# Attention loops of a graph network on one Trainium2 core: the turned logits are shown one round later

## Chip, cores, metric

The kernel runs on one core of one Trainium2 chip. The metric is the device time of one execution in microseconds (us). A run gives the median of several executions; the profiled execution is a separate one with its own time.

## What is computed

Four graph layers over 3125 nodes and 100000 edges sorted by destination, 256 features. The two layers that matter here are attention over the incoming edges of each node. GATv2 is applied twice (the stages `edges1` and `edges2`), GAT with four heads once (`gat_edges`):

```python
# _gatv2, for each edge src -> dst
h = jax.nn.leaky_relu(xl[src] + xr[dst] + eattr @ We, SLOPE)
logits = h @ att
m = jax.ops.segment_max(logits, dst, n)
ex = jnp.exp(logits - m[dst])
denom = jax.ops.segment_sum(ex, dst, n)
out = jax.ops.segment_sum(xl[src] * (ex / denom[dst])[:, None], dst, n)
...
# _L2_gnn_ref, 4 heads
e = jax.nn.leaky_relu(a_src[src] + a_dst[dst], NEG_SLOPE)
m = jax.ops.segment_max(e, dst, num_segments=N)
ex = jnp.exp(e - m[dst])
```

The other stages (a dense product of node pairs for the first and last layer, layer and batch norms, node projections) are untouched.

## The kernel before, in words

The edges are cut into windows of 512 (4 tiles of 128), and windows at block borders are visited twice, so that each of the 220 groups has edges into one block of 128 nodes. The two functions `gatv2_loop` and `gat_loop` run over these groups. Each engine runs its own program, and the engines meet at semaphores alone: one per kind of step, counted up once for each group.

A group passes through a chain of small steps, one of each per group t. Each engine does them in rounds: in round s it takes its steps in a fixed order, each for the group t = s - lag. The list of (lag, step) pairs, handed to `pipelined` (a hardware loop of ten rounds, on TensorE and ScalarE) or to `straight` (written out, on VectorE), sets that order. A step that has to wait stops all that stands behind it on its engine.

In `gatv2_loop` the chain of a group is:

- GpSimd: `gather`, four indirect DMAs (L942) that fetch the source rows of a group into a ring of ten buffers. Before group t it waits for `group_sum` of group t - 10.
- ScalarE: `place` (L1040, L1043) and `mask` (L1050) make the one-hot matrix of destinations and an offset for absent places.
- TensorE: `mix` (L1082, L1085), 16 bf16 matmuls that sum the destination's and the edge's terms.
- VectorE: `sum_inputs` (L954), `dot` (L961), `add_linear` give the logits; `high_part` to `low_part` (L1018) split them into three bf16 parts.
- TensorE: `turn_parts` (L1066), one matmul that transposes the parts. ScalarE: `copy_turned` (L1030), the cast into `rows`.
- TensorE: `show_logits` (L1093, L1095), five matmuls that lay the logits of the group out as nodes by edges in PSUM.
- VectorE: `see` (L967), the maximum of each node, `raise_top`, `drop`, `set_top`. ScalarE: `exponentials` (L1056, L1058).
- TensorE: `flip` (L1072), four fp32 transposes. ScalarE: `copy_weights` (L1034).
- TensorE: `sum_group` (L1104), fp32 matmuls of weights and gathered rows, which also wait for `add_group` of the group before. VectorE: `add_group` (L1013).

ScalarE's order in a round is copy_turned, copy_weights, place, mask, exponentials. `gat_loop` has the same plan with four heads: `mask_first_heads` and `mask_last_heads` (L1367), `turn_parts` (L1361), `show_logits` (L1381, 16 matmuls), `bring_top` (L1355), `mix` (L1409), `flip` (L1390), `sum_group` (L1400) on TensorE; on ScalarE `copy_turned` (L1303), `shrinkage` (L1343), `weigh_late` (L1317), `mask`, `choose` (L1338), `exponentials` (L1308), `weigh_early` (L1317); its gather is L1162.

Of the kernel before, what the change touches and what calls it, by code (L numbers as in the profile page):

```python
# [130 lines left out]
def blocks_on(nc, m, engine):  # L131

    def load(first, n, turn):
        _, values = nc.values_load_multi_w_load_instructions(
            m.tab[0:1, bass.ds(first, n)], engines=[engine], min_val=0, max_val=NB,
            skip_runtime_bounds_check_because="the list of groups has blocks 0 to NB only")
        return values
    return load
# [753 lines left out]
def gatv2_loop(nc, m, name, table, c):  # L892
# [7 lines left out]
    with stage_of(nc, name) as (st, block):  # L900
# [48 lines left out]
        def _(dve):  # L949
# [66 lines left out]
            def low_part(t, u, turn, b):  # L1016
# [1 line left out]
                nc.vector.tensor_tensor(lo, m.rest[:, 0:T], md, ALU.subtract).then_inc(parts, 1)  # L1018


            straight([(2, sum_inputs), (2, dot), (3, see), (2, add_linear), (5, add_group), (3, raise_top),
                            (2, high_part), (3, drop), (2, without_high), (3, set_top), (2, middle_part),
                            (2, low_part)], blocks_on(nc, m, mybir.EngineType.DVE))
            dve.wait_ge(done, NG)

        @block.scalar
        def _(act):
            def copy_turned(t, u, turn, b):
                act.wait_ge(turned, t + 1)
                nc.scalar.copy(rows, turn_ps[:, 0:P]).then_inc(copied, 1)  # L1030

            def copy_weights(t, u, turn, b):
                act.wait_ge(flipped, t + 1)
                nc.scalar.copy(m.prob[:, 0, :], flip_ps[:, :]).then_inc(weights, 1)  # L1034

            def place(t, u, turn, b):
                r = u % R
                act.wait_ge(arrived[r], 16 * n_loads * nth(u, turn, R))

                nc.scalar.activation(m.locrow[r][:, :], m.locrow[r][:, :], ACT.Abs,  # L1040
                                     bias=m.minus_icol[:, 0:1]).then_inc(distance, 1)
                act.wait_ge(distance, t + 1)
                nc.scalar.activation(m.ohT[r][:, :], m.locrow[r][:, :], ACT.Relu, scale=-1.0,  # L1043
                                     bias=m.one[:, 0:1]).then_inc(placed, 1)

            def mask(t, u, turn, b):
                r = u % R
                act.wait_ge(placed, t + 1)

                nc.scalar.activation(m.off[r][:, :], m.ohT[r][:, :], ACT.Identity, scale=BIG,  # L1050
                                     bias=m.minus_big[:, 0:1]).then_inc(masked, 1)

            def exponentials(t, u, turn, b):
                r = u % R
                act.wait_ge(raised, t + 1)
                nc.scalar.activation(m.expT[:, :], shown_ps[:, :], ACT.Exp, bias=m.new[:, 0:1]).then_inc(exps, 1)  # L1056
                act.wait_ge(dropped, t + 1)
                nc.scalar.activation(m.less[r][:, 0:1], m.drop[:, 0:1], ACT.Exp).then_inc(shrink, 1)  # L1058

            pipelined(act, [(3, copy_turned), (4, copy_weights), (0, place), (1, mask), (3, exponentials)])  # L1060

        @block.tensor
        def _(pe):
            def turn_parts(t, u, turn, b):
                pe.wait_ge(parts, t + 1)
                nc.tensor.matmul(turn_ps[:, 0:P], m.parts[:, :], m.ident_bf[:, :], start=True,  # L1066
                                 stop=True).then_inc(turned, 1)

            def flip(t, u, turn, b):
                pe.wait_ge(exps, t + 1)  # L1070
                for j in range(T):
                    mm = nc.tensor.transpose(flip_ps[:, j * P:(j + 1) * P], m.expT[:, j * P:(j + 1) * P], m.ident[:, :])  # L1072
                mm.then_inc(flipped, 1)

            def mix(t, u, turn, b):
                r, q = u % R, u % 2
                pe.wait_ge(placed, t + 1)
                after(pe, summed, t, 2)
                for j in range(T):
                    e = slice(j * P, (j + 1) * P)  # L1080
                    for s in range(3):
                        nc.tensor.matmul(zb[q][:, j, :], m.ohT[r][:, e], blk(m.xr3, b, s * D, (s + 1) * D),  # L1082
                                         start=(s == 0), stop=False)

                    mm = nc.tensor.matmul(zb[q][:, j, :], m.eaT[r][:, e], m.We12[c][:, :], start=False, stop=True)  # L1085
                mm.then_inc(mixed, 1)

            def show_logits(t, u, turn, b):
                r = u % R
                pe.wait_ge(copied, t + 1)  # L1090
                pe.wait_ge(masked, t + 1)

                nc.tensor.matmul(shown_ps[:, :], m.ident_bf[:, :], m.off[r][:, :], start=True, stop=False)  # L1093
                for j in range(T):
                    mm = nc.tensor.matmul(shown_ps[:, j * P:(j + 1) * P], m.tilesel[:, j, :], rows,  # L1095
                                          start=False, stop=(j == T - 1))
                mm.then_inc(shown, 1)

            def sum_group(t, u, turn, b):
                r = u % R  # L1100
                pe.wait_ge(weights, t + 1)
                after(pe, done, t, 1)
                for j in range(T):
                    mm = nc.tensor.matmul(sum_ps[:, 0:WA], m.prob[:, 0, j * P:(j + 1) * P], m.gath[u % RG][:, j, 0:WA],  # L1104
                                          start=(j == 0), stop=(j == T - 1))
                mm.then_inc(group_sum, 1)

            pipelined(pe, [(3, turn_parts), (4, flip), (3, show_logits), (1, mix), (4, sum_group)],
                      blocks_on(nc, m, mybir.EngineType.PE))


def gat_loop(nc, m, name, table):
# [8 lines left out]
    with stage_of(nc, name) as (st, block):  # L1121
# [47 lines left out]
        def _(dve):  # L1169
# [115 lines left out]
            def add_group(t, u, turn, b):  # L1285
# [3 lines left out]
                nc.vector.tensor_tensor(acc, acc, sum_ps[:, 0:WA], ALU.add).then_inc(done, 1)  # L1289


            straight([(2, see), (4, rescale), (1, sum_parts), (2, raise_top), (3, take_top), (1, add_src), (2, top_high_part),
                            (3, sink), (1, leak), (2, drop), (3, bound), (1, high_part), (2, top_without_high),
                            (2, set_top), (1, without_high), (2, top_middle_part), (1, middle_part),
                            (2, top_low_part), (1, low_part), (0, place), (3, weigh), (4, add_group)],
                      blocks_on(nc, m, mybir.EngineType.DVE))
            dve.wait_ge(done, NG)

# [1 line left out]
        def _(act):  # L1300
# [39 lines left out]
            def shrinkage(t, u, turn, b):  # L1340
# [1 line left out]
                act.wait_ge(dropped, t + 1)  # L1342
                nc.scalar.activation(m.less[r][:, 0:H], m.drop[:, 0:H], ACT.Exp).then_inc(shrink, 1)  # L1343

            pipelined(act, [(2, copy_turned), (3, shrinkage), (4, weigh_late), (1, mask), (3, choose), (3, exponentials),
                            (3, weigh_early)])

        @block.tensor
        def _(pe):
# [54 lines left out]
            def mix(t, u, turn, b):  # L1404
# [3 lines left out]
                for j in range(T):  # L1408
# [1 line left out]
                                          blk(m.adst3, b, 0, 3 * H), start=True, stop=True)  # L1410
                mm.then_inc(mixed, 1)

            pipelined(pe, [(2, mask_first_heads), (2, turn_parts), (2, mask_last_heads), (2, show_logits), (3, bring_top),
                           (1, mix), (3, flip), (4, sum_group)],
                      blocks_on(nc, m, mybir.EngineType.PE))


# [544 lines left out]
```

## Time and profile before

| what | value |
|---|---|
| median of 3 runs | 6605.63 us (6604.21 to 6607.28) |
| the profiled execution, its own time | 6665.35 us |
| its span, first to last instruction | 6663.5 us |
| mean granted TensorE clock | 0.923 |
| busy: TensorE matmuls / weight loads | 4911.5 us (74%) / 3594.1 us (54%) |
| busy: VectorE / ScalarE / GpSimd | 4773.6 us (72%) / 3300.0 us (50%) / 3314.7 us (50%) |

Busy is the time in which an engine's records lie; the ends of TensorE's are modelled and not observed. In rows of a timeline the columns are: start in us from the span's start, duration in us, engine, line, operation, out<-in by the program's names, number of instructions merged; in brackets the idle time of the engine before it and what ended that, where the profile tells (`remote`: it doesn't; `issue`: no wait ended there). PE is TensorE, DVE VectorE, ACT ScalarE, POOL GpSimd.

### The profile page before, as it was taken

The page shows a single profiled execution, that of the slowest core. Times are in us where ns is not written, and L with a number is a line of the kernel's source. Part 1 is how long each engine was busy: PE and PEld are TensorE (multiplying, and loading weights), DVE is VectorE, ACT ScalarE, POOL GpSimd, SP SyncE. Part 2 cuts the span into 40 slices and gives each one's busy share as a digit, 9 for nine tenths or more (in the row PEclk, how much of TensorE's full clock was granted, in tenths as well). Part 3 has the DMA queues.
Part 4 walks back from the last instruction along what each step waited for, and adds up shares of the span by engine and source line. Part 5 has one row for each costly group of instructions (what it writes and reads, how often), then busy time and mean ns, then how long its engine had stood idle before and what let it go on. Part 6 is the DMA issues. An engine that isn't in the chain of part 4 may idle for free. (4 is left out here: it accounts for less than half of the span.)

```text
span 6663.5 us, 117090 instructions
## 1 busy us (share of the span) xinstructions
PE 4911.5 (74%) x29984; PEld 3594.1 (54%) x30319; DVE 4773.6 (72%) x18137; ACT 3300.0 (50%) x8374; POOL 3314.7 (50%) x3591
## 2 busy tenths in 40 slices
PE   4999999947777777765777777775477767676589
PEld 2444447816556656643566565563355544454378
DVE  8999992457767777675777767677588777888801
ACT  4777771035555555543555555555355555555510
POOL 3444446545555555535555555552355555555200
PEclk9999999979999999988999999998689898999899
DMA  2233347724444444412444444440333333333164
GB/s 57 62 92 101 111 119 287 287 62 103 105 105 104 104 105 105 104 42 74 105 106 104 104 105 105 104 105 22 88 99 98 96 97 93 95 101 98 51 157 112
DMA packets 606529, 695.56 MB, mean 104 GB/s; under 512 B 243043, under 2 KB 512656, under 8 KB 599802
## 3 DMA queue, kind: packets, MB, share of 16 engines
q0 software_dynamic: 128832, 362.75, 21.6%
q1 hardware_dynamic: 477370, 329.75, 18.3%
q14 instruction: 280, 2.29, 0.1%
q8 instruction: 47, 0.77, 0.0%
HBM read 589.91 MB, written 102.19 MB: 104 GB/s over the span
## 5 line engine op out<-in xcount | busy, mean ns | idle before, releaser
L942 POOL DMA_INDIRECT gath<-table,src_col x880 | 843.3, 958 | 637.3 <-issue 628.2
L942 POOL DMA_INDIRECT h<-table,src_col x880 | 844.9, 960 | 581.3 <-issue 581.3
L1082 PE MATMUL psum<-xr,ohT 128*128 x5280 | 906.7, 296 | 35.1 <-ACT ohT L1043 35.1
L1030 ACT CAST rows<-psum 128x128 bf16<-128x128 f32 x440 | 117.1, 266 | 1337.9 <-remote 847.7
L1241 DVE TENSOR_REDUCE seen<-psum 128x2 f32<-128x1024 f32 x440 | 532.0, 1223 | 282.4 <-remote 158.3
L669 DVE SCALAR_TENSOR_TENSOR xr<-xr,gath,psum 128x259 f32<-128x259 f32 x1440 | 683.3, 474 | 7.4 <-PE psum L655 4.1
L1162 POOL DMA_INDIRECT gath<-table,src_col x440 | 440.1, 1000 | 469.4 <-issue 340.2
L961 DVE SCALAR_TENSOR_TENSOR zs<-zs,mean 128x256 f32<-128x256 f32 x1760 | 643.9, 421 | 0.0
L1082 PEld LDWEIGHTS psum<-xr,ohT 128*128 128x128 bf16 x5280 | 542.2, 106 | 126.9 <-issue 36.7
L1162 POOL DMA_INDIRECT h<-table,src_col x440 | 436.7, 992 | 308.7 <-issue 308.7
L954 DVE TENSOR_TENSOR zs<-psum,gath 128x1024 f32<-128x1024 f32 x220 | 269.4, 1225 | 446.1 <-remote 371.0
L954 DVE TENSOR_TENSOR zs<-psum,h 128x1024 f32<-128x1024 f32 x220 | 269.4, 1225 | 367.1 <-remote 307.2
L1095 PE MATMUL psum<-rows,tilesel 128*128 128x128 bf16 x1760 | 179.9, 228 | 469.6 <-ACT rows L1030 450.3
L1085 PE MATMUL psum<-We,eaT 128*128 128x256 bf16 x1760 | 523.1, 297 | 0.0
L664 DVE TENSOR_SCALAR locrow<-psum,acc 128x128 f32<-128x128 f32 x1440 | 495.2, 344 | 0.3 <-POOL xr L605 0.3
L621 ACT ACTIVATE xr<-irow,gath 128x128 f32<-128x128 f32 x1440 | 460.1, 390 | 56.6 <-PEq L173 6.3
L655 PE MATMUL psum<-zs,locrow 128*128 128x259 f32 x1440 | 416.8, 414 | 71.4 <-DVE xr L669 21.9
L1104 PE MATMUL psum<-h,prob 128*128 128x257 f32 x1760 | 430.6, 388 | 48.2 <-DVE acc L1013 46.7
L1104 PE MATMUL psum<-gath,prob 128*128 128x257 f32 x1760 | 436.7, 393 | 15.4 <-DVE acc L1013 14.5
L1093 PEld LDWEIGHTS psum<-off,ident_bf 128*128 128x128 bf16 x440 | 42.3, 96 | 741.7 <-ACT rows L1030 736.8
L698 PE MATMUL psum<-h,xr 128*128 128x256 f32 x1900 | 416.2, 381 | 5.9 <-DMA xr<-pairs 5.9
L698 PEld LDWEIGHTS psum<-h,xr 128*128 128x128 f32 x1900 | 363.2, 191 | 57.8 <-DMA xr<-pairs 7.7
(328 smaller groups left out, 12200.0 us busy)
## 6 DMA issues: line engine op xcount, KB each, us to landing
locrow<-g_locb SPq DMA_DIRECT2D x660, 128.0 KB
pairs<-xr SPq DMA_DIRECT2D x640, 115.5 KB
xr<-pairs SPq DMA_DIRECT2D x13, 1716.0 KB
gath<-table,src_col POOLq DMA_INDIRECT x1320
h<-table,src_col POOLq DMA_INDIRECT x1320
xr<-pairs SPq DMA_DIRECT2D x25, 832.0 KB
acc<-pairs SPq DMA_DIRECT2D x12, 1716.0 KB
xr<-pairs SPq DMA_DIRECT2D x13, 1584.0 KB
```

What stands on the lines that cost most here:

```text
L621: ins = nc.scalar.activation(gap[u % 2][:, j, :], m.irow[:, :], ACT.Abs, bias=col(t["low"], t4 * 4 + j))
L664: nc.vector.tensor_scalar(pick[u % 8], numbers, t["key"][:, g:g + 1], None, ALU.is_equal).then_inc(keyed, 1)
L669: nc.vector.scalar_tensor_tensor(kept[:, u, 0:EXTRA + 3], kept[:, (u - 1) % HELD, 0:EXTRA + 3], t["same"][:, g:g + 1], m.ps[u % 4][:, 0:EX ...
L698: mm = nc.tensor.matmul(sums_of(m, hb), lhs(i, hb), m.h[:, db, :], start=False, stop=(db == NB - 1 and (hb % 2 == 1 or hb == n - 1)))
L942: pool.indirect_dma_start(m.gath[r][:, j, :], None, table, bass.IndirectOffsetOnAxis(m.src_col[r][:, j:j + 1], 0)).then_inc(gathered[r], 16)
L954: nc.vector.tensor_tensor(m.zs[q][:, :, :], zb[q], m.gath[u % RG][:, :, 0:D], ALU.add).then_inc(summed, 1)
L961: ins = nc.vector.scalar_tensor_tensor(m.zs[q][:, j, :], m.zs[q][:, j, :], 0.0, m.att_relu[:, :], ALU.max, ALU.mult, accum_out=m.dots[:, j ...
L1082: nc.tensor.matmul(zb[q][:, j, :], m.ohT[r][:, e], blk(m.xr3, b, s * D, (s + 1) * D), start=(s == 0), stop=False)
L1085: mm = nc.tensor.matmul(zb[q][:, j, :], m.eaT[r][:, e], m.We12[c][:, :], start=False, stop=True)
L1104: mm = nc.tensor.matmul(sum_ps[:, 0:WA], m.prob[:, 0, j * P:(j + 1) * P], m.gath[u % RG][:, j, 0:WA], start=(j == 0), stop=(j == T - 1))
L1162: pool.indirect_dma_start(m.gath[r][:, j, :], None, table, bass.IndirectOffsetOnAxis(m.src_col[r][:, j:j + 1], 0)).then_inc(gathered[r], 16)
L1241: ins = nc.vector.tensor_reduce(m.seen[:, 2 * q:2 * q + 2], m.psum[:, 2 * q:2 * q + 2, :], AX.X, ALU.max)
```

## The change

All steps from `show_logits` on are taken one round later on every engine, and on TensorE `turn_parts` moves behind `show_logits`: what is turned and cast in one round is shown in the next. In `gatv2_loop` `turn_parts` also moves behind `mix`, next to `sum_group`. ScalarE's and VectorE's orders within a round stay as they are; only the groups differ.

```diff
@@ gatv2_loop, VectorE @@
-            straight([(2, sum_inputs), (2, dot), (3, see), (2, add_linear), (5, add_group), (3, raise_top),
-                            (2, high_part), (3, drop), (2, without_high), (3, set_top), (2, middle_part),
+            straight([(2, sum_inputs), (2, dot), (4, see), (2, add_linear), (6, add_group), (4, raise_top),
+                            (2, high_part), (4, drop), (2, without_high), (4, set_top), (2, middle_part),
                             (2, low_part)], blocks_on(nc, m, mybir.EngineType.DVE))
@@ gatv2_loop, ScalarE @@
-            pipelined(act, [(3, copy_turned), (4, copy_weights), (0, place), (1, mask), (3, exponentials)])
+            pipelined(act, [(3, copy_turned), (5, copy_weights), (0, place), (1, mask), (4, exponentials)])
@@ gatv2_loop, TensorE @@
-            pipelined(pe, [(3, turn_parts), (4, flip), (3, show_logits), (1, mix), (4, sum_group)],
+            pipelined(pe, [(5, flip), (4, show_logits), (1, mix), (3, turn_parts), (5, sum_group)],
                       blocks_on(nc, m, mybir.EngineType.PE))
@@ gat_loop, VectorE @@
-            straight([(2, see), (4, rescale), (1, sum_parts), (2, raise_top), (3, take_top), (1, add_src), (2, top_high_part),
-                            (3, sink), (1, leak), (2, drop), (3, bound), (1, high_part), (2, top_without_high),
-                            (2, set_top), (1, without_high), (2, top_middle_part), (1, middle_part),
-                            (2, top_low_part), (1, low_part), (0, place), (3, weigh), (4, add_group)],
+            straight([(3, see), (5, rescale), (1, sum_parts), (3, raise_top), (4, take_top), (1, add_src), (3, top_high_part),
+                            (4, sink), (1, leak), (3, drop), (4, bound), (1, high_part), (3, top_without_high),
+                            (3, set_top), (1, without_high), (3, top_middle_part), (1, middle_part),
+                            (3, top_low_part), (1, low_part), (0, place), (4, weigh), (5, add_group)],
@@ gat_loop, ScalarE @@
-            pipelined(act, [(2, copy_turned), (3, shrinkage), (4, weigh_late), (1, mask), (3, choose), (3, exponentials),
-                            (3, weigh_early)])
+            pipelined(act, [(2, copy_turned), (4, shrinkage), (5, weigh_late), (1, mask), (4, choose), (4, exponentials),
+                            (4, weigh_early)])
@@ gat_loop, TensorE @@
-            pipelined(pe, [(2, mask_first_heads), (2, turn_parts), (2, mask_last_heads), (2, show_logits), (3, bring_top),
-                           (1, mix), (3, flip), (4, sum_group)],
+            pipelined(pe, [(3, mask_first_heads), (3, mask_last_heads), (3, show_logits), (2, turn_parts), (4, bring_top),
+                           (1, mix), (4, flip), (5, sum_group)],
```

TensorE in the hardware loop of `edges1`, before: from the sum of one group to the show of another, with the semaphores that each row waits for.

```order
L1104 MATMUL psum<-h,prob 128x257 [waits edges1_done,edges1_weights]
L1104 MATMUL psum<-h,prob 128x257 x3
L1066 MATMUL psum<-ident_bf,parts 128x128 [waits edges1_parts]
L1072 MATMUL psum<-ident,prob 128x128 [waits edges1_exps]
L1072 MATMUL psum<-ident,prob 128x128 x3
L1093 MATMUL psum<-off,ident_bf 128x512 [waits edges1_masked,edges1_copied]
L1095 MATMUL psum<-rows,tilesel 128x128 x4
```

And the same engine and place of the changed kernel, from the last matmuls of `mix` on.

```order
L1082 MATMUL psum<-xr3,ohT 128x256 x3
L1085 MATMUL psum<-We12_1,eaT1 128x256
L1066 MATMUL psum<-ident_bf,parts 128x128 [waits edges1_parts]
L1104 MATMUL psum<-h,prob 128x257 [waits edges1_done,edges1_weights]
L1104 MATMUL psum<-h,prob 128x257 x3
L1072 MATMUL psum<-ident,prob 128x128 [waits edges1_exps]
L1072 MATMUL psum<-ident,prob 128x128 x3
L1093 MATMUL psum<-off,ident_bf 128x512 [waits edges1_masked,edges1_copied]
L1095 MATMUL psum<-rows,tilesel 128x128 x4
```

The transpose L1066 has moved from between the sum and the flips to between `mix` and the sum.

ScalarE in the hardware loop of `edges1`, the same rows in both kernels; shown is the changed one.

```order
L1030 CAST rows<-psum 128x128 [waits edges1_turned]
L1034 COPY prob<-psum 128x512 [waits edges1_flipped]
L1040 ACTIVATE locrow<-locrow,minus_icol 128x512 [waits const_split]
L1043 ACTIVATE ohT<-locrow,one 128x512 [waits edges1_distance]
L1050 ACTIVATE off<-ohT,minus_big 128x512 [waits edges1_placed]
L1056 ACTIVATE prob<-psum,new 128x512 [waits edges1_raised]
L1058 ACTIVATE less<-drop 128x1 [waits edges1_dropped]
```

Nothing moved here: the cast L1030 still opens the round, and its transpose on TensorE now ends later in the round. (The name of the semaphore at L1040 is that of an earlier stage with the same number; it is the arrival of the loads.)

TensorE in the hardware loop of `gat_edges`, before.

```order
L1367 MATMUL psum<-off,ident_bf 128x512 x2
L1361 MATMUL psum<-ident_bf,parts 128x128
L1367 MATMUL psum<-off,ident_bf 128x512 x2
L1381 MATMUL psum<-rows,edgesel 128x128 x16
L1355 MATMUL psum<-new,ohT 128x12 x4
```

And in the changed kernel.

```order
L1367 MATMUL psum<-off,ident_bf 128x512 x4
L1381 MATMUL psum<-rows,edgesel 128x128 x16
L1361 MATMUL psum<-ident_bf,parts 128x128
L1355 MATMUL psum<-new,ohT 128x12 x4
L1406 REGISTER_ALU
```

Here the transpose L1361 has moved behind the 16 matmuls of the show.

## Rows read from the trace of the kernel before

**Rows 1.** Windows by stage: busy us of each engine (instructions), granted clock, DMA share, GB/s.
```profile
1440.00:2890.00 1450.00, 1042.74 (x7127) 843.59 (x7233) 989.81 (x4258) 731.24 (x1494) 844.12 (x880) 0.93 0.45 105
3100.00:4550.00 1450.00, 1057.05 (x7263) 858.78 (x7373) 1010.04 (x4345) 741.78 (x1521) 826.27 (x862) 0.93 0.44 103
4719.00:6290.00 1571.00, 1075.69 (x8894) 763.02 (x9004) 1232.69 (x5056) 825.05 (x2852) 876.73 (x880) 0.89 0.37 95
```

**Rows 2.** Pauses in the steady part of edges1: us, times, longest.
```profile
ACT rows L1030 <- remote: 361.6, 109, 5.3
```

**Rows 3.** Timeline of POOL: first and last burst of edges1's and gat_edges's steady rounds.
```profile
1511.51 0.97 POOL L942 DMA_INDIRECT gath<-table,src_col  x1 [1.87 <-issue]
2883.92 0.98 POOL L942 DMA_INDIRECT h<-table,src_col  x1 [1.82 <-issue]
4786.02 0.94 POOL L1162 DMA_INDIRECT gath<-table,src_col  x1 [16.38 <-issue]
6240.48 1.02 POOL L1162 DMA_INDIRECT h<-table,src_col  x1 [2.44 <-issue]
```

**Rows 4.** Timeline of edges1 between two POOL bursts, POOL idle.
```profile
1500.06 0.39 PE L1093 MATMUL psum<-off,ident_bf 128*128 128x512 bf16 x1
1500.51 0.49 PE L1082 MATMUL psum<-xr,ohT 128*128 x3
1502.26 1.90 PE L1104 MATMUL psum<-gath,prob 128*128 128x257 f32 x8
1504.07 0.23 PE L1066 MATMUL psum<-ident_bf,parts 128*128 128x128 bf16 x1
1504.13 0.60 PE L1072 MATMUL psum<-ident,prob 128*128 128x128 f32 x4
1504.33 0.27 ACT L1030 CAST rows<-psum 128x128 bf16<-128x128 f32 x1 [0.24 <-PE psum L1066]
1504.94 0.95 POOL L942 DMA_INDIRECT gath<-table,src_col  x1 [15.08 <-issue]
```

**Rows 5.** Timeline of a steady round of edges1 (three engines and POOL).
```profile
2605.45 0.27 ACT L1030 CAST rows<-psum 128x128 bf16<-128x128 f32 x1 [2.05 <-PE psum L1066]
2606.16 0.95 POOL L942 DMA_INDIRECT h<-table,src_col  x1 [1.74 <-issue]
2608.09 0.67 ACT L1056 ACTIVATE prob<-psum,new 128x512 f32<-128x512 f32 x1
2609.70 0.22 PE L1066 MATMUL psum<-ident_bf,parts 128*128 128x128 bf16 x1
2611.89 1.23 DVE L954 TENSOR_TENSOR zs<-psum,gath 128x1024 f32<-128x1024 f32 x1 [3.33 <-remote]
2612.02 0.27 ACT L1030 CAST rows<-psum 128x128 bf16<-128x128 f32 x1 [3.17 <-remote]
2612.18 0.59 ACT L1034 COPY prob<-psum 128x512 f32<-128x512 f32 x1
2612.73 0.95 POOL L942 DMA_INDIRECT h<-table,src_col  x1 [1.86 <-issue]
```

**Rows 6.** Timeline of a later round of edges1: burst start, DVE's next read.
```profile
2639.16 0.98 POOL L942 DMA_INDIRECT gath<-table,src_col  x1 [1.85 <-issue]
2643.48 1.23 DVE L954 TENSOR_TENSOR zs<-psum,h 128x1024 f32<-128x1024 f32 x1 [1.89 <-PE psum L1085]
```

**Rows 7.** Timeline of a steady round of gat_edges.
```profile
5339.85 0.95 POOL L1162 DMA_INDIRECT gath<-table,src_col  x1 [1.85 <-issue]
5341.02 0.27 ACT L1303 CAST rows<-psum 128x128 bf16<-128x128 f32 x1
5341.29 1.30 ACT L1317 ACTIVATE gath<-gath,ex 128x65 f32<-128x65 f32 x5
5342.69 1.99 PE L1400 MATMUL psum<-gath,prob 128*128 128x260 f32 x8
5345.74 0.59 ACT L1338 COPY prob<-psum 128x512 f32<-128x512 f32 x1 [2.54 <-remote]
```

## The prediction

> **What bounds the kernel now.** I read the windows by stage first, because the change touches three loops and nothing else. Each loop of 220 groups is one window: 1450 us for edges1, 1450 for edges2, 1571 for gat_edges, so two thirds of the span [rows 1]. No engine is full in them: in edges1 TensorE's records fill 1042.74 of 1450 us, VectorE's 989.81, ScalarE's 731.24, GpSimd's 844.12 [rows 1]. So a chain bounds the round, and the next view is the period. In edges1 the gathers of a group start at 1511.51 for the first steady group and at 2883.92 for the 209th after it: 6.57 us a round [rows 3]. edges2's window has the same length and I give it the same period. gat_edges takes (6240.48 - 4786.02) / 209 = 6.96 us [rows 3].
>
> The timeline then shows what the 6.57 us consist of, in two stretches. Where GpSimd issues no gathers, TensorE goes from one `show_logits` (1500.06) to the next `turn_parts` (1504.07) in 4.01 us, and ScalarE's cast of the turned matrix starts 0.26 us after it, at 1504.33 [rows 4]. That is a natural round of about 4.3 us. In the steady state the same `turn_parts` is recorded at 2609.70, but the cast that waits for it starts only at 2612.02, after 3.17 us of idle time [rows 5]; 109 such pauses add up to 361.6 us in edges1 [rows 2]. DVE, which waits for `mix`, starts at 2611.89, nearly at the same moment [rows 5]. So completions of TensorE become visible late, in bunches, and the bunch comes at a fixed place: the cast starts 5.86 us after the start of the POOL burst at 2606.16 [rows 5]. In another round the completion of `mix` came 4.32 us after the start of the burst, at 2643.48 against 2639.16 [rows 6]. The gather's issue closes the ring: POOL waits for the group_sum of ten groups back and starts its next burst at 2612.73, 0.71 us after the bunch [rows 5]. The cycle is burst, late completions, next burst. I call the delay a hold; what in the chip makes it, the trace doesn't tell.
>
> One rule of the Trainium skill speaks against such a hold (SBUF — State Buffer, section "SBUF: two separate sides"): engine ports and DMA ports are disjoint, and TensorE never waits for anyone. The 3.17 us of the cast and the 3.33 us of DVE [rows 5] aren't explained by it, and I go by the rows. What the rule would make of the time is the first rival.
>
> **The change part by part.** Nothing is added to the work: the same matmuls, casts and DMAs, in another order.
>
> *edges1, edges2, what is removed.* `show_logits` no longer waits for a cast whose `turn_parts` stands just ahead of it. From `turn_parts` to the cast that is 0.26 us [rows 4], and the cast's own 0.27 follows. The gain is at most about 0.5 us a round, and only where nothing else ends last.
>
> *edges1, edges2, what is added.* `turn_parts` of a round now stands behind `mix` on TensorE and right ahead of `sum_group`. ScalarE's order is unchanged: its round begins with the cast, and behind the cast are queued the copy of the weights, which `sum_group` of this same round needs, the two activations that place the next group, the mask, and the exponentials, which the first instruction of TensorE's next round, `flip`, needs. So ScalarE's whole round and most of TensorE's now follow one another. Step by step, from the start of a cast:
> - ScalarE to the end of the exponentials: 2605.45 to 2608.09 + 0.67, 3.31 us [rows 5].
> - Hand-over to TensorE: 0.1, an estimate; the 0.26 us from 1504.07 to 1504.33, which hold a matmul of 0.23 as well, bound it [rows 4].
> - `flip`: the four transposes take 0.60 as recorded, pipelined [rows 4]; 0.5 until the next can start.
> - `show_logits`: 1500.06 to 1500.51, 0.45 [rows 4].
> - `mix`: 1500.51 to 1502.26, 1.75 [rows 4].
> - `turn_parts` to the next cast: 0.26 [rows 4].
>
> That sums to 6.37 us, and it is a floor. On the side: the copy of the weights ends 0.75 after the cast's start (2612.02 to 2612.18 + 0.59) [rows 5], so TensorE stands idle 0.85 us between `turn_parts` and `sum_group`, where before other matmuls covered the copy; `sum_group` takes 1.90 [rows 4], so it ends 2.75 after the cast's start, and POOL's burst follows 0.78 later (1502.26 + 1.90 to 1504.94) [rows 4], at 3.53. Without a hold the next cast would come at 6.37, that is 2.84 us into the burst.
>
> There the hold meets the chain. Its cost is not a row of this trace for this order, so it is bounded from both sides: zero, if a completion 2.84 us into a burst gets through; and 5.86 - 2.84 = 3.02 us, if it waits as the cast does now [rows 5]. Between them I take the row that is nearest in kind, the completion of `mix` at 4.32 us into a burst [rows 6], since `turn_parts` now follows `mix` directly. The cast then starts 4.35 us into the burst, and the round takes 3.53 + 4.35 = 7.88 us, against 6.57: +1.31. Over 2 x 210 steady rounds that is +550 us.
>
> *gat_edges.* Here `show_logits` moves ahead of `turn_parts` too, but the matmuls between `turn_parts` and `sum_group` stay. ScalarE runs the late weighing after the cast: it ends at 5341.29 + 1.30 = 5342.59, TensorE's `sum_group` takes 1.99 [rows 7], so its natural end is about 5344.7, and the bunch comes at 5345.74 [rows 7], 5.89 us after the start of the burst at 5339.85. One us is spare. TensorE's turn may come 0.3 us later, behind the show; the spare covers it. The round stays with burst and hold, 5.89 and about 0.8 to the next burst (0.78 in [rows 4]), 6.7 us, under the mean of 6.96; the difference is rounds that come late now, of which the looser chain may save some. I take -20 us, between -50 (all of 6.96 - 6.7 over 210 rounds) and +60 (the 0.3 us shown in full).
>
> *Depth.* Each loop has one more round of filling and draining: between 0 and 3 x 7.9, I take +15.
>
> *The clock.* The granted clock is 0.93 in edges1, with TensorE busy for 72% of the window, and 0.89 in gat_edges at 68% [rows 1]. At 7.88 us a round the same 1042.74 us of matmuls fill about 60%, so I expect it to be granted the lower level (1.2 GHz) more often. At 0.05 less, a tenth more of the rounds have their 2.7 us of flip, show, mix and turn doubled; half of it hidden in the hold, that is 0.14 x 420 = +60 us. The cover is the hold; without it the price is double.
>
> The Trainium skill (TensorE: Matmul & The Clock Gate, section "What's actually happening") says that the lower level is the default and activity lifts it; two windows with less activity and less clock agree [rows 1].
>
> Sum: +550 - 20 + 15 + 60 = +605 us on the profiled execution's own 6665.35 us (span 6663.5). The median of the runs is 6605.63, 0.9% lower, so I scale: +600, and 7205; I say **7210 us**.
>
> **The rivals.**
> - *No hold in the new order* (the other side). The round is 6.37, or 0.20 less than now: -84 us, with the other terms and the clock in full about 6540 us. For it: the completion of the `turn_parts` at 1504.07 is seen at once [rows 4], and TensorE will have less queued in a burst than now. Against: 109 pauses [rows 2]. By the rule of the Trainium skill's page SBUF — State Buffer (same section) this would be the only outcome. It decides at one point: the cast must start before 3.04 us into the burst (6.57 - 3.53), only 0.20 after its natural place. Chance 0.12.
> - *Full hold.* The cast waits for the end of the burst as now, 5.86: the round is 9.39, +2.82, +1184 us, about 7800 us. For it: that is what the cast does today [rows 5]. Against: the burst then begins later against the chain and `mix` got through at 4.32 [rows 6]. Chance 0.10.
> - *A weak hold*, 0.3 to 0.9 us, so that the round is 6.7 to 7.3 and the time 6650 to 6950 us. The hold may depend on how much TensorE has queued, and it has less queued now, since it waits for the weights. Chance 0.18, of which 0.03 is no measurable change, the case that the ring of burst and group_sum alone sets the pace at 6.57.
> - *As forecast*, with 6950 to 7600 us as its own range: 0.60.
>
> The range of 6600 to 7620 us leaves out the first two. A difference of 0.2% is about what a measurement of this kernel can tell from none. Faster 0.12, same 0.03, slower 0.85.
>
> **What the profile after would show.** In edges1: bursts of POOL 7.9 us apart in the timeline; `sum_group` (L1104) idle about 0.8 us before it, released by ScalarE's copy L1034; `flip` (L1072) released by the exponentials L1056; the cast L1030 still idle before it, released by L1066; ScalarE without a pause between cast and exponentials; `show_logits` with no wait for the cast. In gat_edges: about 6.9 us, `show_logits` no longer released by L1303. Wrong would be: bursts at 6.6 us or less in edges1, or `sum_group` starting right behind `turn_parts`. The prediction fails if the hold has another size, or if ScalarE gets to its copy of the weights before the cast.

## The result and the profile after

The changed kernel takes 7260.42 us (median of 4 runs, 7250.64 to 7275.36) where the kernel before takes 6606.45 beside it: a ratio of 1.0979, 95% interval 1.0959 to 1.0999. It is slower by 650 us; the forecast was 7210. The total came out, but not in the way that the sum had it: edges1 and edges2 cost less than forecast, and gat_edges, which was to gain 20 us, lost 160.

The windows by stage of the kernel after (same columns as [rows 1]; the stretches are longer, since the loops are):
```profile
1440.00:3200.00 1760.00, 1203.58 (x7580) 928.87 (x7580) 1054.34 (x4463) 760.28 (x1573) 842.83 (x886) 0.92 0.35 86
3400.00:5200.00 1800.00, 1201.83 (x7567) 925.72 (x7565) 1121.58 (x4616) 792.21 (x1658) 832.85 (x879) 0.91 0.34 84
5400.00:7000.00 1600.00, 999.38 (x8240) 752.05 (x8238) 1132.57 (x4645) 761.48 (x2645) 746.72 (x757) 0.87 0.33 87
```
TensorE's records fill 68% of edges1 instead of 72%, at nearly the same clock. The period follows from POOL's timeline, which stands here with the bursts of group 10 and of the last group, 209 rounds later, in edges1 and in gat_edges:
```profile
1516.33 0.95 POOL L942 DMA_INDIRECT gath<-table,src_col  x1 [25.41 <-issue]
3106.02 0.95 POOL L942 DMA_INDIRECT h<-table,src_col  x1 [2.43 <-issue]
5237.74 0.95 POOL L1162 DMA_INDIRECT gath<-table,src_col  x1 [17.13 <-issue]
6852.23 0.95 POOL L1162 DMA_INDIRECT h<-table,src_col  x1 [1.74 <-issue]
```
That is 7.61 us a round in edges1 and 7.73 in gat_edges (edges2: 7.57). Before it was 6.60, 6.96 and 6.60 [rows 3, 4]; from 1504.94 to 2883.92 there are 209 rounds; the prediction counted as many from 1511.51, where there are 208, and had 6.57. So edges1 and edges2 cost +1.0 us a round, together some +415 us, and gat_edges +0.77, +160 us. Filling the first two loops takes 10 us more each.

The pauses of edges1, of three kinds after (us, times, longest):
```profile
ACT rows L1030 <- PE psum L1066: 486.5, 133, 6.6
ACT rows L1030 <- remote: 279.2, 50, 7.2
PE psum L1104 <- ACT prob L1034: 186.6, 76, 5.2
```
and the second kind of pause of the cast before, which [rows 2] leave out:
```profile
ACT rows L1030 <- PE psum L1066: 246.0, 100, 3.4
```
Both kinds together, the cast waited 607.6 us before (2.9 a round) and 765.7 after (4.0 a round, in a window of 1450 us), and TensorE's `sum_group` (L1104) now waits for ScalarE's copy of the weights (L1034). But a round of 7.6 us is not what one finds in the timeline. Two rounds of edges1, next to each other:
```profile
2584.85 0.95 POOL L942 DMA_INDIRECT gath<-table,src_col  x1 [0.82 <-issue]
2587.31 0.22 PE L1066 MATMUL psum<-ident_bf,parts 128*128 128x128 bf16 x1
2590.94 0.27 ACT L1030 CAST rows<-psum 128x128 bf16<-128x128 f32 x1 [6.27 <-remote]
2591.75 3.68 PE L1104 MATMUL psum<-gath,prob 128*128 128x257 f32 x8 [4.22 <-ACT prob L1034]
2596.20 0.94 POOL L942 DMA_INDIRECT gath<-table,src_col  x1 [6.65 <-issue]
2597.88 0.22 PE L1066 MATMUL psum<-ident_bf,parts 128*128 128x128 bf16 x1
2598.14 0.27 ACT L1030 CAST rows<-psum 128x128 bf16<-128x128 f32 x1 [3.79 <-PE psum L1066]
2598.95 2.00 PE L1104 MATMUL psum<-gath,prob 128*128 128x257 f32 x8 [0.84 <-issue]
2601.73 0.95 POOL L942 DMA_INDIRECT gath<-table,src_col  x1 [0.82 <-issue]
```
In the first, the turn stands 2.46 us into the burst and the cast sees it 6.09 us into it, when the burst is over; `sum_group` then runs its 8 matmuls in 3.68 us instead of 2.00, and the round is 11.35 us. In the second the turn stands 1.68 us into the burst, the cast sees it after 0.26, and the round is 5.53. Of edges1's 209 rounds 89 take 6.3 to 6.7 us, 23 take 5 to 6, and 57 take over 8.5, 10.45 on the mean. The forecast had one hold, until 4.35 us into the burst, in every round. Measured, of the 210 steady casts of edges1, 125 start within 0.6 us of their turn, 53 start 0.6 to 2.0 us after it, most of them while the burst still runs (about 3.5 and 4.3 us into it), and 32 start 3.3 to 4.6 us after it, when the burst is over.

In gat_edges the same happens, and worse:
```profile
5509.57 1.31 POOL L1162 DMA_INDIRECT h<-table,src_col  x1 [2.02 <-issue]
5515.09 1.16 POOL L1162 DMA_INDIRECT h<-table,src_col  x1 [0.45 <-issue]
5515.90 0.22 PE L1361 MATMUL psum<-ident_bf,parts 128*128 128x128 bf16 x1
5519.06 0.95 POOL L1162 DMA_INDIRECT h<-table,src_col  x1 [0.30 <-issue]
5521.28 0.27 ACT L1303 CAST rows<-psum 128x128 bf16<-128x128 f32 x1 [6.37 <-remote]
5521.55 1.30 ACT L1317 ACTIVATE h<-h,ex 128x65 f32<-128x65 f32 x5
5522.95 3.81 PE L1400 MATMUL psum<-h,prob 128*128 128x260 f32 x8 [6.41 <-issue]
```
Two bursts follow with 0.45 us between them; the turn (L1361) stands at 5515.90, 6.3 us after the start of the first and early in the second, and is seen by the cast 5.38 us later, after the end of both. Behind the cast stands the late weighing (L1317), behind that `sum_group` (L1400). Before, the cast hardly waited in this loop: of the 210 from group 10 on, 36 stood idle for over 0.1 us, 20.6 us in all. After, 196 do, and the pauses of gat_edges have two large rows for it (window 5240 to 6855):
```profile
ACT rows L1303 <- remote: 315.1, 54, 7.3
ACT rows L1303 <- PE psum L1361: 310.8, 116, 5.1
```

### The profile page after: what moved, and what is told of

It is laid out like the page before. It is cut to its first block and busy times, and to the rows that moved or that the text cites. A ratio compares the mean times of both kernels' runs of the same rounds, so it can differ in the third digit from the quotient of the medians.

```text
span 7273.6 us, 117508 instructions
## 1 busy us (share of the span) xinstructions
PE 5100.9 (70%) x30318; PEld 3702.6 (51%) x30319; DVE 4777.4 (66%) x18137; ACT 3274.8 (45%) x8374; POOL 3290.0 (45%) x3591
## 5 line engine op out<-in xcount | busy, mean ns | idle before, releaser
L1030 ACT CAST rows<-psum 128x128 bf16<-128x128 f32 x440 | 117.5, 267 | 1895.3 <-PE psum L1066 1151.7
L1082 PE MATMUL psum<-xr,ohT 128*128 x5280 | 819.7, 278 | 44.1 <-issue 22.6
L1104 PE MATMUL psum<-gath,prob 128*128 128x257 f32 x1760 | 526.5, 451 | 412.7 <-ACT prob L1034 270.8
L1104 PE MATMUL psum<-h,prob 128*128 128x257 f32 x1760 | 495.0, 430 | 319.5 <-issue 177.3
L967 DVE TENSOR_REDUCE seen<-psum 128x1 f32<-128x512 f32 x440 | 304.4, 692 | 580.4 <-PE psum L1095 499.1
L1104 PEld LDWEIGHTS psum<-gath,prob 128*128 128x128 f32 x1760 | 368.3, 220 | 517.9 <-ACT prob L1034 294.0
L1104 PEld LDWEIGHTS psum<-h,prob 128*128 128x128 f32 x1760 | 347.4, 207 | 415.9 <-issue 261.8
L1400 PE MATMUL psum<-gath,prob 128*128 128x260 f32 x880 | 279.5, 472 | 315.2 <-issue 238.6
L1085 PE MATMUL psum<-We,eaT 128*128 128x256 bf16 x1760 | 488.0, 277 | 0.0
L1072 PE MATMUL psum<-ident,prob 128*128 128x128 f32 x1760 | 310.0, 303 | 252.1 <-ACT prob L1056 132.5
L986 DVE CAST parts<-lg 128x4 bf16<-128x4 f32 x440 | 89.8, 204 | 591.0 <-PE psum L1066 294.8
```

## The experiments

My theory after these traces: (1) with the turn late on TensorE and its cast first on ScalarE, one round of ScalarE and most of one of TensorE follow each other, in gat_edges too; (2) bursts of GpSimd's gathers hold the turn's completion. The rivals: the extra lag costs by itself; the late turn costs through VectorE's `high_part`, which waits for it; the gathers have no part in it; gat_edges has no part in it. The experiments ran on four chips, called A to D here. Each time is compared with the kernel before as it ran on the same chip. "Holds" is short for late completions.

**One loop kind at a time (chip A).** The diff's hunks for edges1 and edges2 alone, of which this is the core:
```diff
-            pipelined(act, [(3, copy_turned), (4, copy_weights), (0, place), (1, mask), (3, exponentials)])
+            pipelined(act, [(3, copy_turned), (5, copy_weights), (0, place), (1, mask), (4, exponentials)])
-            pipelined(pe, [(3, turn_parts), (4, flip), (3, show_logits), (1, mix), (4, sum_group)],
+            pipelined(pe, [(5, flip), (4, show_logits), (1, mix), (3, turn_parts), (5, sum_group)],
```


> The change in edges1 and edges2 alone, gat_edges as before. From the trace of after, the two loops take +1.01 and +0.97 us a round and 20 us more to fill: +435, so about 7040 us, if the loops don't influence each other. The prediction's own sum for these loops, +550 with a colder clock on top, would be 7180 to 7220 us. If the cost sat in gat_edges, it would be 6605 us.

and the hunks for gat_edges alone:
```diff
-            pipelined(pe, [(2, mask_first_heads), (2, turn_parts), (2, mask_last_heads), (2, show_logits), (3, bring_top),
+            pipelined(pe, [(3, mask_first_heads), (3, mask_last_heads), (3, show_logits), (2, turn_parts), (4, bring_top),
```


> The change in gat_edges alone. The prediction took -20 us for this loop, with +60 as its worst: 6555 to 6665 us. The trace of after says +0.77 us a round, about +160 us: near 6765 us, with rounds of 5 and of 10 to 12 us side by side and the cast L1303 waiting for the turn L1361.

On this chip the kernel before took 5670.52 us, a seventh less than on the others. The first took 6260.10 (ratio 1.1038, 1.102 to 1.1057: +590 us), the second 5702.14 (1.0057, 1.004 to 1.0074: +32 us). The time levels expected were those of another chip; of the differences, +590 is near the prediction's sum for these loops only by coincidence, since here no completion is late, and gat_edges costs a fifth of what the trace of after showed. Why, the timelines say. In the kernel with gat_edges alone changed, edges1 is the code of before, and its bursts of group 10 and of the last group stand here:
```profile
1491.34 0.96 POOL L942 DMA_INDIRECT gath<-table,src_col  x1 [0.30 <-issue]
2562.20 0.95 POOL L942 DMA_INDIRECT h<-table,src_col  x1 [0.30 <-issue]
```
5.12 us a round, with 0.30 us before a gather: four gathers of 0.95 with their gaps are 5.0, so POOL itself sets the pace, and no completion comes late. With edges1 and edges2 changed, the casts of group 10 and of the last, and a round between them:
```profile
1518.95 0.27 ACT L1030 CAST rows<-psum 128x128 bf16<-128x128 f32 x1 [2.90 <-PE psum L1066]
2004.94 0.22 PE L1066 MATMUL psum<-ident_bf,parts 128*128 128x128 bf16 x1
2005.20 0.27 ACT L1030 CAST rows<-psum 128x128 bf16<-128x128 f32 x1 [2.90 <-PE psum L1066]
2006.01 2.00 PE L1104 MATMUL psum<-gath,prob 128*128 128x257 f32 x8 [0.84 <-ACT prob L1034]
2007.85 0.67 ACT L1056 ACTIVATE prob<-psum,new 128x512 f32<-128x512 f32 x1
2008.57 0.65 PE L1072 MATMUL psum<-ident,prob 128*128 128x128 f32 x4 [0.56 <-ACT prob L1056]
2011.25 0.22 PE L1066 MATMUL psum<-ident_bf,parts 128*128 128x128 bf16 x1
2011.50 0.27 ACT L1030 CAST rows<-psum 128x128 bf16<-128x128 f32 x1 [2.90 <-PE psum L1066]
2868.75 0.27 ACT L1030 CAST rows<-psum 128x128 bf16<-128x128 f32 x1 [2.21 <-PE psum L1066]
```
This is the serial round of the prediction, without a hold: cast to the end of the exponentials 3.32 (forecast 3.31), flip 0.05 later, 2.68 more to the turn, 0.25 to the next cast: 6.30 us, where 6.37 were forecast. Every cast sees its turn after 0.26 though POOL is gathering. The mean is 6.46, (2868.75 - 1518.95) / 209, since every tenth round takes about 8.06 us (casts at 2076.22 and 2084.28): the loops are unrolled ten groups deep, and it comes once in each turn. The forecast had left these out. Against the 5.12 of before, 6.46 is +1.34 us a round, 563 us over the two loops; the rest is mostly the longer filling of both loops (12 us from the first cast to that of group 10 in edges1, 17 in edges2).

**The cast at the end (chip A).** edges1 and edges2 as after, but
```diff
-            pipelined(act, [(3, copy_turned), (5, copy_weights), (0, place), (1, mask), (4, exponentials)])
+            pipelined(act, [(5, copy_weights), (0, place), (1, mask), (4, exponentials), (3, copy_turned)])
```


> edges1 and edges2 changed as in after, with one edit: ScalarE's cast of the turned matrix goes from the head of its round to the end, behind the exponentials. gat_edges as before. Theory of the place: the copy of the weights, and with it sum_group of the same round, no longer stands behind the held cast; the ring of burst and bunch alone is left, 6.57 us a round and some us of filling: 6560 to 6660 us. Rival, a turn late on TensorE costs by itself, through VectorE's high_part that waits for it: 6800 us or more. Rival, the lag itself: about 7000 us.

It took 5669.56 us: ratio 0.9998 (0.9989 to 1.0008). With one call moved in a list all +590 us are gone, while the lag, the late turn and VectorE's wait for it stay. The place of the cast is the cause of the loss. One thing this run can't show: POOL's own pace of 5.12 us stands over the 4.70 that the round takes without gathers (below), so a cost of the lag or of `high_part` under 0.4 us a round would be hidden here. The runs on chips B and C are the test for that.

**The whole change again, and the turn first (chip B).** First the kernel after, unchanged:

> The changed kernel once more, beside the kernel before on the same chip. In the last call the kernel before took 5670.52 us where the shown runs have 6606, and its relatives showed rounds of 5.1 us in edges1: there the hold of TensorE's completions is absent. If this call meets the same conditions: the two parts add up, +590 and +32 us, so 6290 us. If it meets those of the first runs: 7260 us and before 6606.

It took 7230.40 us against 6668.11, ratio 1.0839 (1.0803 to 1.0875): on chip B completions are late, as they were in the first runs. Then edges1 and edges2 with the longer lags, but the turn where it was. That needs two turned matrices at a time, and the turn waits for the cast of the group before (shortened):
```diff
-            pipelined(pe, [(5, flip), (4, show_logits), (1, mix), (3, turn_parts), (5, sum_group)],
+            pipelined(pe, [(3, turn_parts), (5, flip), (4, show_logits), (1, mix), (5, sum_group)],
+                after(pe, copied, t, 1)
-                nc.scalar.copy(rows, turn_ps[:, 0:P]).then_inc(copied, 1)
+                nc.scalar.copy(m.rows[:, (u % 2) * P:(u % 2 + 1) * P], turn_ps[:, (u % 2) * P:(u % 2 + 1) * P]
+                               ).then_inc(copied, 1)
```


> edges1 and edges2 with the longer lags kept, but turn_parts back at the head of TensorE's round; the turned matrix and its cast copy are double buffered for that, and turn_parts waits for the cast before it. gat_edges as before. Theory of the place: the time is that of the kernel before within 0.5% and 30 us of filling, 5660 to 5700 us where before takes 5670, 6400 to 6650 where it takes 6606. Rival, the lag itself costs: near the run with the change in edges1 and edges2 alone, 6260 or 7040 us.

6712.62 us, ratio 1.0071 (1.0049 to 1.0092): 0.7% above before, against 8.4% for the whole change, though above the 6400 to 6650 us that were expected; what the 45 us are isn't shown. Its bursts of group 10 and the last in edges1:
```profile
1507.24 1.06 POOL L941 DMA_INDIRECT gath<-table,src_col  x1 [18.23 <-issue]
2899.86 1.03 POOL L941 DMA_INDIRECT h<-table,src_col  x1 [1.03 <-issue]
```
6.66 us a round, 0.06 above the first trace's 6.60. So under holds too, the lag is not what costs.

**No gathers on GpSimd (chip B).** Both kernels, with this in the three loops, where SyncE's program issues it (shortened). The rows fetched are not the listed ones, so both kernels compute something else; only their times are used:
```diff
-                    pool.indirect_dma_start(m.gath[r][:, j, :], None, table,
-                                            bass.IndirectOffsetOnAxis(m.src_col[r][:, j:j + 1], 0)
-                                            ).then_inc(gathered[r], 16)
+                    at = (t * T + j) % NB * P
+                    sp.dma_start(m.gath[r][:, j, :], table[at:at + P, :]).then_inc(gathered[r], 16)
```


> The kernel before with each indirect gather of GpSimd replaced by a plain load of 128 rows of the table from SyncE's queue (as many bytes; the rows fetched are not the listed ones, so the output is another). GpSimd issues nothing in the loops. Theory that the burst of gathers is what the rounds go by, through the ring and through the hold: edges1 falls from 5.12 us a round (6.60 in the first trace) to between 4.5, VectorE's busy time of a round, and 4.8, and gat_edges to its VectorE's 5.5: 5350 to 5550 us on any chip, without late completions. Rival, completions are late for another reason: where before takes 6606 us, this stays above 6000.

> The changed kernel with the same replacement (the output is another here too). Theory of the serial round: its 6.37 us are ScalarE's and TensorE's own work end to end, and no gather is in them, so edges1 keeps 6.3 us a round and the time stays at 6200 to 6300 us, 750 to 900 above the other kernel with plain loads. Rival, the changed order costs because of the gathers' ring: it falls with them, to under 5900 us.

The kernel before falls from 6668.11 to 5488.90 us (ratio 0.8227, 0.821 to 0.8244), the kernel after from 7230.40 to 6304.75 (0.9451 of before, 0.9433 to 0.947): on a chip with late completions, none is late any more: each of the 420 steady casts of edges1 and edges2 starts 0.25 to 0.27 us after its turn, in both. The casts of group 10 and of the last in edges1, first of the kernel before with plain loads:
```profile
1511.09 0.27 ACT L1029 CAST rows<-psum 128x128 bf16<-128x128 f32 x1 [0.83 <-PE psum L1065]
2493.74 0.27 ACT L1029 CAST rows<-psum 128x128 bf16<-128x128 f32 x1 [1.33 <-PE psum L1065]
```
then of the kernel after with plain loads, and its window of this stretch:
```profile
1530.84 0.27 ACT L1029 CAST rows<-psum 128x128 bf16<-128x128 f32 x1 [2.90 <-PE psum L1065]
2880.76 0.27 ACT L1029 CAST rows<-psum 128x128 bf16<-128x128 f32 x1 [2.21 <-PE psum L1065]
1531.00:2881.00 1350.00, 1016.81 (x6969) 795.26 (x7074) 963.15 (x4167) 701.58 (x1460) 0.00 (x0) 1.00 0.40 104
```
4.70 and 6.46 us a round. The serial round is the same 6.46 as on chip A, with POOL idle and as many bytes moved. What remains of 7.4 to 7.6, about 1 us a round, is the hold and what it does to the clock.

**Half the burst (chip C).** Two of a group's four gathers on GpSimd, two as plain loads of other rows than the listed ones, in both kernels (shortened):
```diff
-                for j in range(T):
+                for j in range(T // 2):
                     pool.indirect_dma_start(m.gath[r][:, j, :], None, table,
...
+                for j in range(T // 2, T):
+                    at = (t * T + j) % NB * P
+                    sp.dma_start(m.gath[r][:, j, :], table[at:at + P, :]).then_inc(other[r], 16)
```

> The kernel before with two of the four gathers of a group on GpSimd and two replaced by plain loads of table rows from SyncE's queue (other rows, so another output). The burst is 2.2 us instead of 4.7. Theory that completions are held for the length of the burst: a round needs 0.75 + 2.2 + 0.9 = 3.9 us for the ring, less than VectorE's 4.5, so the round is 4.5 to 5.0 us and the time 5450 to 5750 us on any chip. Rival, any indirect gather in the loop delays completions by some us: above 6200 where before takes about 6640.

> The changed kernel with the same halving (another output too). Theory: the turn completes 2.84 us after the start of the burst by the chain, the bunch comes 3.1 after it (2.2 + 0.9), so the held time shrinks from 1 to 3 us to at most 0.3, and the round is 6.3 to 6.6: 6300 to 6450 us on any chip. Rival as above: about 7000 us where before takes about 6640.

5632.58 us against 6613.33 (ratio 0.8516, 0.8497 to 0.8534) and 6506.07 (0.9839, 0.9818 to 0.9859). The first is as expected, the second 56 us over its range. A round of edges1 in the second, from its burst of two:
```profile
2210.18 0.94 POOL L949 DMA_INDIRECT h<-table,src_col  x1 [4.28 <-issue]
2211.43 0.95 POOL L949 DMA_INDIRECT h<-table,src_col  x1 [0.30 <-issue]
2212.63 0.22 PE L1074 MATMUL psum<-ident_bf,parts 128*128 128x128 bf16 x1
2213.05 0.27 ACT L1038 CAST rows<-psum 128x128 bf16<-128x128 f32 x1 [3.05 <-PE psum L1074]
```
The turn now stands 0.25 us behind the burst's end, and is seen after 0.42 us instead of 0.26, in round after round: 6.45 us a round, 6.69 on the mean. With half the burst, a round of edges1 is 4.93 us in the order of before (6.60 with the whole, in the first trace) and 6.69 in the new one (7.6 there; 7.4 on chip B). In both kernels all but some ten of 210 turns of edges1 now stand outside the burst, so these runs show that the delay goes when the overlap goes; how a shorter burst delays a turn inside it they hardly show.

**Repairs in all three loops (chip C).** The cast at the end, in gat_edges
```diff
-            pipelined(act, [(2, copy_turned), (4, shrinkage), (5, weigh_late), (1, mask), (4, choose), (4, exponentials),
-                            (4, weigh_early)])
+            pipelined(act, [(4, shrinkage), (5, weigh_late), (1, mask), (4, choose), (4, exponentials), (4, weigh_early),
+                            (2, copy_turned)])
```


> All three loops changed as in after, but ScalarE's cast of the turned matrix stands at the end of its round: behind the exponentials in edges1 and edges2, behind the early weighing in gat_edges. Where before takes 5670 us: 5660 to 5720. Where before takes about 6640: theory of the place, nothing that sum_group needs stands behind the held cast, so rounds of 6.6 in edges1 and about 6.9 in gat_edges, 6600 to 6730 us. Rival, the turn late on TensorE costs under the hold by itself (VectorE's high_part waits for it): 6850 us or more.

and the turn first in TensorE's list in all three, in gat_edges so:
```diff
-            pipelined(pe, [(3, mask_first_heads), (3, mask_last_heads), (3, show_logits), (2, turn_parts), (4, bring_top),
+            pipelined(pe, [(2, turn_parts), (3, mask_first_heads), (3, mask_last_heads), (3, show_logits), (4, bring_top),
```

> All three loops with the longer lags of after, but turn_parts at the head of TensorE's round in each, the turned matrix and its cast copy double buffered. Theory of the place: gat_edges loses the +0.97 us a round that the change gave it in the last call and stays at 6.95; with edges1 and edges2 as measured there (6.6), 6650 to 6740 us where before takes about 6640, 5670 to 5720 where it takes 5670. Rival, gat_edges pays for the lag: 6850 or more.

The first took 6645.88 us (ratio 1.0049, 1.003 to 1.0069), the second 6736.18 (1.019, 1.0167 to 1.0213). The bursts of group 10 and of the last of gat_edges, first with the cast at the end:
```profile
4790.19 0.95 POOL L1162 DMA_INDIRECT gath<-table,src_col  x1 [16.14 <-issue]
6234.00 0.94 POOL L1162 DMA_INDIRECT h<-table,src_col  x1 [1.66 <-issue]
```
then with the turn first:
```profile
4803.74 1.03 POOL L1161 DMA_INDIRECT gath<-table,src_col  x1 [18.99 <-issue]
6305.40 0.94 POOL L1161 DMA_INDIRECT h<-table,src_col  x1 [2.14 <-issue]
```
6.91 and 7.19 us a round. Moving the cast alone takes gat_edges back to the 6.96 of before; with the turn first, 0.2 us stay that I can't place. VectorE's `high_part` still waits for a late turn in the first kernel, in edges1 from 1700 to 2500 us most of all here:
```profile
DVE parts L986 <- remote: 104.4, 31, 5.6
```
The whole kernel is 0.5% above before all the same, so that this wait and the lag matter little is shown under holds as well. No version that computes the same as the kernel before beats it.

**gat_edges alone under holds (chip D).** The second diff of this section once more.

> The change in gat_edges alone, once more. Where before takes about 5670 us: 5700 again. Where before takes 6600 to 6670, with completions held: the cast L1303 opens ScalarE's round, the late weighing and then sum_group of the same round stand behind it, and the turn now stands behind the 18 matmuls of masks and show, so its completion falls into the burst: +0.8 to +1.0 us a round, 6760 to 6870 us, with rounds of over 9 us among those of 5 to 6.5. By the prediction's step for this loop, a spare of 1 us that covers the later turn: -20 to +60 us.

6856.58 us against 6666.37, ratio 1.0287 (1.027 to 1.0305): +190 us where chip A gave +32. Its bursts of group 10 and the last of gat_edges:
```profile
4784.21 0.95 POOL L1162 DMA_INDIRECT gath<-table,src_col  x1 [17.39 <-issue]
6424.22 0.97 POOL L1162 DMA_INDIRECT h<-table,src_col  x1 [1.96 <-issue]
```
7.85 us a round; 64 of 209 are over 8.5 us, 11.1 on the mean. Edges1 and edges2, unchanged here, take the 6.60 of before. The prediction's step for this loop is refuted by this run alone.

## Why the prediction was right in its total

- *The ring and the hold as the bound of before:* right. Without GpSimd's gathers the round of edges1 falls from 6.6 to 4.70 us, near the 4.3 read between bursts [rows 4].
- *The serial round:* right, term by term: 6.30 against 6.37, and TensorE idle 0.84 us ahead of `sum_group` against 0.85. The view's other signs are there too: flip released by the exponentials, no pause on ScalarE between cast and exponentials. The mean of 6.46, with its long tenth round, was missed.
- *The price of the hold in it:* the mechanism right, the size off. The term was 7.88 - 6.37 = 1.51 us a round, taken from one row of `mix` [rows 6]. Measured, the casts of edges1 start 0.85 us later than at once on the mean (179 us over 210 rounds), and hold and clock together add 7.6 - 6.46 = 1.1 us (0.9 on chip B). The row was no typical delay: more than half of the turns are seen within 0.6 us, a quarter in the course of the burst, and 32 of 210 after its end. With the step up from 6.60 this made +415 us where +550 stood. The bursts 7.9 us apart, which the text named as its sign, are a mean over rounds from 5.5 to over 11 us.
- *gat_edges:* this is the step that failed, "The round stays with burst and hold". It costed `turn_parts` as 0.3 us later against a spare of 1 us, and did not follow its completion. The cast opens ScalarE's round, the late weighing and `sum_group` are queued behind it: the chain that the prediction had found in the other loops exists here as well. Before, the turn stood ahead of the last masks and the show, and the cast of the row shown follows without idle time [rows 7]. Behind the show it falls into a burst. Measured: +0.77 us a round, +160 us, against -20; alone on chip D, 6.96 to 7.85 us a round and +190 us; and with the cast moved behind, 6.91 us again.
- *The clock:* direction right, size off: 0.92 and 0.91 instead of 0.88. A long hold costs the next `sum_group` 1.7 us (3.68 against 2.00, above), but most rounds have no long hold. Summed, the `sum_group`s of edges1 take 73 us more than at 2.00 each, 0.35 us a round where the forecast had 0.14: the clock fell less than forecast, but its price was not half hidden, since it comes behind the hold.
- *Depth:* +15 forecast; the first two loops fill 10 us later each, gat_edges 0.6.

So the sum, +605, is near the +610 of the two profiled spans by luck, because two errors met: the rounds of edges1 and edges2 with their clock gave +415 instead of +610, gat_edges +160 instead of -20; filling and what lies around the loops the other 35, instead of 15. The rival *no hold* was priced against a before that stays held. (Its time was also summed wrongly: 6605.63 - 84 - 20 + 15 + 60 is 6577 us, or 6637 with the clock term doubled, and not 6540.) Chip A shows what no hold means: both kernels are faster, before at POOL's own pace of 5.12, and the change costs more, 10%, since a serial round of 6.46 no longer has a slow ring to compare with. What decided its sign, 3.04 us into the burst, was the wrong comparison.

## What to carry to other kernels

When a producer is moved later in one engine's list and its consumer stays at the head of another's, ask what of the same round is queued behind that consumer, in every loop that is edited, and follow the completion to the end of that chain before calling anything spare. The repair was in the consumer's list, not in the producer's: one call moved to the end of each list gave back all of the loss on one chip (edges1 and edges2), and all but 0.5% on another (all three loops). And a delay that one row shows at one size can have several: price it by its distribution over the rounds, not by one row. Here its mean was 0.85 us where a single row gave 1.51.

## What the runs showed of the hardware

- TensorE's completions come late while GpSimd issues indirect gathers, on three of the chips A to D (before: 6668.11, 6613.33 and 6666.37 us; on A 5670.52) and in the first runs. One 2.46 us into a burst of 4.7 us was seen 3.6 us after it stood, one at 1.68 after 0.26. Completions of ScalarE and VectorE were not late where I looked: in edges1 of after, `sum_group` starts 0.05 to 0.13 us after the end of ScalarE's copy of the weights in all 134 rounds where it waited for a copy that ended within a burst, and in edges1 of before ScalarE's exponentials start 0.04 us or less after VectorE's L980 in all 54 such rounds. Replacing the gathers by SyncE's plain loads of as many bytes ends it (6668.11 to 5488.90). Whether it is GpSimd's issue or the scattered reads themselves isn't told apart by this, and why a chip does it or not stays open.
- The Trainium skill (SBUF — State Buffer, section "SBUF: two separate sides") has TensorE and ScalarE wait for no one at their SBUF ports. Chip A's traces agree (0.26 us from turn to cast in the midst of a burst); in the trace of after the same hand-over takes 3.63 us (2587.31 to 2590.94). Either the wait is elsewhere than at these ports, or the rule doesn't hold here; the runs can't say which.
- The granted clock in edges1 of after, ahead of and around another slow `sum_group` (2608.60, 3.61 us, behind 4.19 us of idle time on TensorE):
```profile
2600.00:2608.00 8.00, 3.85 (x31) 2.87 (x29) 3.01 (x16) 1.76 (x6) 4.70 (x5) 1.00 0.48 128
2608.00:2613.00 5.00, 3.77 (x10) 2.50 (x11) 2.71 (x13) 3.17 (x7) 0.01 (x1) 0.66 0.08 19
```
In the second stretch it falls to 0.66 on the mean, so two thirds of it run at the lower level, 1.2 GHz, and the rest at 2.4 GHz. With no late completions the clock of edges1 was 1.00 in the kernel after (the window with plain loads).
